# One bound per routed expert: every second expert's weights bounded by sums of absolute values on ScalarE, the others by the largest value on VectorE

## The reference

```python
H = einsum('btd,od->bto', x, W)
delta = einsum('btr,bor->bto', einsum('btd,brd->btr', x, A[idx]), Bm[idx]) * scalings[idx]
c = H + delta
shared = sum over 2 experts of gelu(c @ Wsh_up) @ Wsh_down
probs = softmax(c @ W_router); gate = the 2 largest of 16 probabilities
routed = sum over 16 experts of (gelu(c @ Wrt_up) * gate) @ Wrt_down
out = x + shared + routed
```

## Time and profile before

| | before |
|---|---|
| median of 3 runs | 685.81 us (685.29 to 686.54) |
| span of the profiled execution, first to last instruction | 679.9 us |
| PE, DVE, ACT, POOL busy | 627.5, 457.4, 327.2, 222.6 us |
| mean granted TensorE clock | 0.974 of full speed |
| bytes moved, mean rate | 135.68 MB, 200 GB/s |

### The profile page before, as it was taken

One profiled execution on the slowest core, in us unless ns is written; L12 is line 12 of the kernel. 1 busy time (PEld: TensorE's weight loads), 2 busy tenths in 40 slices (PEclk: granted clock), 3 DMA queues, 4 the chain that ended last, 5 costly groups with the idle time before them and its releaser, 6 DMA issues.

```text
span 679.9 us, 13742 instructions
## 1 busy us (share of the span) xinstructions
PE 627.5 (92%) x4115; PEld 428.4 (63%) x4117; DVE 457.4 (67%) x900; ACT 327.2 (48%) x480; POOL 222.6 (33%) x288
## 2 busy tenths in 40 slices
PE   4998999999989758889999999999999999989794
PEld 2465656566657435556777777777777777665561
DVE  2779999999974998525555555555555554688674
ACT  1333224677775743464555555555555554333230
POOL 1000000101012742373333333333333306777771
PEclk9997999999998988999999999999999999999898
DMA  7688994343334312165555555555555539989966
GB/s 275 281 312 286 374 346 168 123 157 142 132 127 128 124 63 93 32 217 171 159 159 169 161 154 159 164 168 157 156 159 167 164 107 377 366 301 362 369 205 248
DMA packets 49765, 135.68 MB, mean 200 GB/s; under 512 B 6160, under 2 KB 6288, under 8 KB 47312
## 3 DMA queue, kind: packets, MB, share of 16 engines
q1 hardware_dynamic: 38304, 97.93, 39.1%
q0 software_dynamic: 11440, 37.50, 20.0%
HBM read 86.38 MB, written 49.02 MB: 199 GB/s over the span
## 4 chain that ended last, share of the span: by engine, by line
PE 53%; DVE 17%; POOL 12%; issue 7%; DMA 7%; ACT 1%; SPq 0%; DVEq 0%; POOLq 0%; ACTq 0%
PE bank L1412 15%; PE bank L1393 14%; POOL rtw L608 9%; PE bank L1249 7%; PE bank L1377 5%; DVE lot_max L906 5%; DMA act_in<-xT 3%; PE bank L1402 2%; PE bank L1327 2%; PE bank L1257 2%; PE bank L1274 2%; DMA region<-xc_dram,slot_idx 2%; PE bank L1238 1%; DVE x_max L947 1%; PE bank L1265 1%
## 5 line engine op out<-in xcount | busy, mean ns | idle before, releaser
L1129 DVE SCALAR_TENSOR_TENSOR region<-bank,scale,region 128x512 f16<-128x512 f32 x79 | 59.2, 751 | 128.7 <-ACT region L809 128.7
L1393 PE MATMUL bank<-rtw,region 128*128 x948 | 116.4, 273 | 0.0
L1412 PE MATMUL bank<-rtw,tmp 128*128 x474 | 115.2, 379 | 0.6 <-DVE tmp L1137 0.6
L1393 PEld LDWEIGHTS bank<-rtw,region 128*128 128x128 f16 x948 | 92.8, 98 | 10.1
L1340 PE MATMUL bank<-shw,hid 128*128 128x512 f16 x384 | 91.3, 397 | 8.3 <-DVE rtw L1193 7.7
L574 POOL DMA_INDIRECT region<-xc_dram,slot_idx x79 | 77.1, 976 | 61.3 <-POOL slot_idx L571 61.3
L1327 PE MATMUL bank<-act_in,shw 128*128 128x256 f16 x768 | 89.4, 277 | 2.9 <-ACT tmp L756 1.7
L1327 PEld LDWEIGHTS bank<-act_in,shw 128*128 128x128 f16 x768 | 75.8, 100 | 16.0 <-ACT tmp L756 2.2
L816 ACT ACTIVATE region<-bank,un_dn 128x512 f32<-128x512 f32 x79 | 54.3, 687 | 57.3 <-PE bank L1412 54.8
L608 POOL DMA_INDIRECT rtw<-r_dram,row_idx x64 | 70.0, 1093 | 27.6 <-issue 14.8
L1340 PEld LDWEIGHTS bank<-shw,hid 128*128 128x128 f16 x384 | 38.4, 102 | 56.4 <-issue 10.0
(11 more groups left out here) (157 smaller groups left out, 910.0 us busy)
## 6 DMA issues: line engine op xcount, KB each, us to landing
r_dram<-region SPq DMA_DIRECT2D x79, 256.0 KB
rtw<-rt_w SPq DMA_DIRECT2D x16, 1024.0 KB, 7.4
act_in<-xT SPq DMA_DIRECT2D x16, 512.0 KB, 3.8
xc_dram<-rows SPq DMA_DIRECT2D x16, 512.0 KB, 3.7
xcT_dram<-hid SPq DMA_DIRECT2D x16, 512.0 KB, 2.8
rtw<-x_rows SPq DMA_DIRECT2D x16, 512.0 KB, 5.4
rtw<-xcT_dram SPq DMA_DIRECT2D x13, 512.0 KB, 6.1
out<-rtw SPq DMA_DIRECT2D x9, 512.0 KB, 5.6
```

The costliest lines, as they stand in the source:

```text
L1129: nc.vector.scalar_tensor_tensor(xgT[s][:, 1], R_XT[s][:].rearrange("p (k t) -> p k t", k=HK), col(scale, C_ALL).bitcast(F32), xgT[s][:, 0 ...
L1393: last = mm(R_UP[s][:, 0:D], xgT[s][:, xp, k, :], rtw[:, bass.ds(e, 1), w0:w0 + D].rearrange("p a d -> p (a d)"), start=(k == 0 and n == 0 ...
L1412: last = mm(R_DN[s][:], midT[s][:, xp, m, :], rtw[:, bass.ds(e, 1), w0:w0 + H].rearrange("p a h -> p (a h)"), start=(m == 0 and n == 0), s ...
```

## The change

The bounds of the odd experts are no longer the largest absolute values, found on DVE, but the sums of absolute values, taken on ACT (`lot_sums`: two `Abs` activations of 128 x 1024 with a sum along the row; the 16-bit absolute values themselves are written to a place that isn't used at the time). A sum of absolute values is never below the largest of them, so the scale stays a valid one, and the power of two is a smaller one. ACT counts its bounds in a semaphore of its own, `lot_sum_ready`, and SP waits for bound n in the semaphore of the engine that makes it. ACT's loop over steps 4 to 7 is written out. DVE's eight bounds are spread anew over its steps.

```diff
--- before.py
+++ after.py
@@ -249,8 +249,8 @@
 
         w_adapters, w_mask, w_cond, w_shared = sem("w_adapters"), sem("w_mask"), sem("w_cond"), sem("w_shared")
         w_loaded = sems("w_loaded", 4)
-        lot_max_ready, largest_ready, reduced, scale_ready, un_ready = (
-            sem("lot_max_ready"), sem("largest_ready"), sem("reduced"), sem("scale_ready"), sem("un_ready"))
+        lot_max_ready, lot_sum_ready, largest_ready, reduced, scale_ready, un_ready = (
+            sem("lot_max_ready"), sem("lot_sum_ready"), sem("largest_ready"), sem("reduced"), sem("scale_ready"), sem("un_ready"))
         w_half, w_split, c_chunk_ready = sem("w_half"), sem("w_split"), sem("c_chunk_ready")
         condT_loaded, condT_half, actT_ready = sems("condT_loaded"), sem("condT_half"), sem("actT_ready")
         hid_half, hid_ready = sem("hid_half"), sem("hid_ready")
@@ -372,7 +372,7 @@
                         sp.wait_ge(lin_split, 2)
                     if n + 5 == E_RT:
                         sp.wait_ge(w_split, 2)
-                    sp.wait_ge(lot_max_ready, n + 1)
+                    sp.wait_ge(lot_sum_ready if n % 2 else lot_max_ready, n // 2 + 1)
                     sp.dma_start(arrived(n + 5), rt_w[:, bass.ds(n + 4, 1), :].rearrange("p a n -> p (a n)")).then_inc(w_loaded[r], 16)
 
             for i in range(E_RT // 4 - 1):
@@ -664,6 +664,19 @@
                     last = nc.scalar.activation(src, src, ACT.Copy, scale=by)
                 last.then_inc(condT_half, 1)
 
+            def lot_sums(e):
+                i, r = e // 4, e % 4
+                act.wait_ge(w_loaded[r], 16 * (i + 1))
+                if e > E_RT // 2:
+                    act.wait_ge(w_split, 1)
+                if e > 1:
+                    act.wait_ge(lot_sum_ready, e // 2)
+                for u in range(2):
+                    place = rtw[:, 0 if e > E_RT // 2 else E_RT - 1, u * WU:(u + 1) * WU]
+                    last = nc.scalar.activation(place, arrived(e + 1)[:, u * WU:(u + 1) * WU], ACT.Abs,
+                                                accum_out=lot_max[:, u, e:e + 1])
+                last.then_inc(lot_sum_ready, 1)
+
             def high_linear(dst, src, n):
                 nc.scalar.activation(dst, src, ACT.Copy, scale=col(scale, n).bitcast(F32)).then_inc(lin_half, 1)
 
@@ -708,17 +721,25 @@
             cond_step(0, 1, first=True)
             high_x(3, 1)
             cond_T(1, 0, 1, first=True)
+            lot_sums(1)
             act.wait_ge(scale_ready, 2)
             high_shared(0)
             cond_rows(1, 0)
             high_x(4, 0)
             cond_T(2, 1, 0)
+            lot_sums(3)
             high_shared(1)
             cond_rows(1, 1)
-            with act.Fori(2, A_HALF // 2) as i:
+            for i in range(2, A_HALF // 2):
                 for s in range(2):
                     high_x(2 * i + s + 1, 1 - s)
-                    cond_step(i, s)
+                    cond_T(2 * i + s - 1, i - 1 + s, 1 - s)
+                    if i == 2:
+                        lot_sums(5 + 2 * s)
+                    else:
+                        for e in (9 + 4 * s, 11 + 4 * s):
+                            lot_sums(e)
+                    cond_rows(i, s)
             def routed_step(i, s, more=True):
                 c = 2 * i + s
                 if more:
@@ -1008,17 +1029,18 @@
             link(nc.vector.tensor_scalar(mask[:], mask[:], w_to_a[:], None, ALU.mult))
             x_largest(1, 0)
             x_scales(2, 0)
-            search_step(0, 1, [(0, 0), (0, 1)], masked=True)
+            search_step(0, 1, [(0, 0)], masked=True)
             scales(2, SH_UP, RT_UP)
-            search_step(1, 0, [(0, 2), (0, 3), (1, 0)])
-            search_step(1, 1, [(1, 1), (1, 2), (1, 3)])
+            search_step(1, 0, [(0, 2)])
+            search_step(1, 1, [(1, 0)])
             for i in range(2, A_HALF // 2):
                 for s in range(2):
-                    search_step(i, s, [(i, 2 * s), (i, 2 * s + 1)])
+                    search_step(i, s, [(1 + s, 2 - 2 * s)] if i == 2 else [(2, 2)] if s == 0 else [(3, 0), (3, 2)])
                     if i == 2:
                         low_shared(s)
             dve.wait_ge(c_chunk_ready, EARLY)
-            dve.wait_ge(lot_max_ready, E_RT)
+            dve.wait_ge(lot_max_ready, E_RT // 2)
+            dve.wait_ge(lot_sum_ready, E_RT // 2)
             nc.vector.tensor_reduce(largest[:, RT_UP:RT_DN + 1], lot_max[:], AX_X, ALU.max)
             nc.vector.tensor_reduce(col(largest, C_EARLY), c_chunk[:, 0:EARLY], AX_X, ALU.max).then_inc(largest_ready, 1)
             scales(3, RT_UP, C_ALL)
```

## The result

| | before | after |
|---|---|---|
| median of 4 runs each | 686.17 us (685.29 to 687.32) | 704.33 us (699.75 to 705.74) |
| ratio | | 1.0269, 95% interval 1.0225 to 1.0313 |
| span of the profiled execution | 679.9 us | 703.7 us |
| VectorE, ScalarE busy | 457.4, 327.2 us | 439.2, 343.3 us |
| start of PE's step 2, of step 15 | 37.00, 187.78 | 38.03, 207.15 |

The account below looks back on a forecast made before the run. A transfer relay, then DVE, then PE were taken to bound the kernel; a closed loop of 14.55 us per turn delays the scales by 13.6 us, plus 1.6 for the clock: 15.2 on 685.81 gives 701.0 us, range 693 to 709.

Parts of the forecast that it names:

- What bounds the kernel, and that only the end of the scales moves: Relay of transfers, then DVE, then PE at 10.86 us; the scales' end at 117.7 us shifts everything later.
- Parts 1 to 3 of the loop: Steps 2 to 6: x arrival to end of `cond_T` 5.94 us, `lot_sums` 2.2, SP's issues 0.4.
- Part 4, the transfer: In the loop, the next x chunk lands 6.0 us after issue behind a load; ends 5.0 and 7.1.
- x 9: Last x transfer, with two loads ahead: 8.8 us, landing at 122.6 us instead of 103.4.
- The clock: Around steps 8 and 9 PE's lower clock costs 1.6 of 3.5 us; inside the loop the loss is hidden.
- Rival D: Low clock makes PE join the loop, period 17 or 18 us, some 712 us in all; chance 0.14.
- The time around the span: Time outside the profiled span: 5.9 us, taking 695.1 to 701.0.
- B: Faster: x transfers are short and the relief of DVE counts, 678 to 684 us; chance 0.05.
- C: No difference: loop period near 12 us as loads and transfers overlap fully, 686 us; chance 0.03.
- A: The closed loop over steps 2 to 6 as summed, 693 to 709 us; chance 0.78.
- The signs: Expected in the changed trace, such as SP's loads behind ACT's sums, scales at about 131 us, DVE busy 18 us less.

Follow-up runs that it names:

- e9: Changed kernel, but in the first six chunks SP stores rows and transpose only once the x transfer ahead has landed: 695.52 us, ratio to before 1.0161.
- e1: Changed kernel, but SP issues the next x chunk ahead of the two bound waits and the two expert loads: 679.93 us, ratio to before 0.9916.
- e3: Changed kernel, but SP waits for the arrival of load n, not bound n, before issuing load n+4: 675.88 us, ratio to before 0.9877.
- e2: Changed kernel, but behind the wait for the odd bound SP issues the next x chunk before the 1 MB load: 685.09 us, ratio to before 0.9996.

## Why the prediction was right

It gave 701.0 us in a range of 693 to 709; measured are 704.3. The mechanism was the one forecast, but the number is nearer than its parts deserve. The scales were forecast 13.6 us later and came 19.4 us later, or 18.3 without the later start of step 2; and 1.6 us were put on the clock, which cost nothing. Without that term the sum is 699.4. By its own steps:

- *What bounds the kernel, and that only the end of the scales moves.* Right. The scales end 19.4 us later, of which 1.03 were there at the start of step 2 already. From the scales to the transposes of step 9 are 8.63 us in both kernels (117.73 to 126.36, 137.09 to 145.72), and the steps behind are 10.87 us. The stretch grew by 18.3 us and the time by 18.2. The 1.03 us are no more than what the start of step 2 differs by between profiles.
- *Parts 1 to 3 of the loop.* 5.94, 2.2 and 0.4 us were predicted and measured. The issue of x 4 was forecast at 45.1 us and came at 46.14, of which 1.03 is the later start.
- *Part 4, the transfer.* The term that was mis-sized: 6.0 us predicted, 7.03, 6.79, 6.87, 6.85 and 6.97 measured, a mean of 6.9. Five of them make 4.5 us. I had reckoned with the load ahead and taken the other load as gone, which it was, but left the two stores behind x out; e9 puts 1.1 us on them. The trace of before had a near case that the sum didn't use, an x transfer with a load 0.4 us ahead and both stores within 1 us behind (a second load, issued at 52.78, was still under way). Its line in the chain, and the two stores among SP's issues:

```profile
55.67 7.02 DMA act_in<-xT
...
56.15 0.43 SPq L361 DMA_DIRECT2D xc_dram<-rows  x1
56.62 0.54 SPq L363 DMA_DIRECT2D xcT_dram<-hid  x1
```

The x transfer of the earlier trace rows, 7.1 us, which I had taken as the upper end because of traffic ahead of it, also had a store 0.5 us behind it (issued at 67.21, against 66.73). The Trainium skill says in "DMA: Bandwidth & Descriptors", "Queues, rings and completion order", that descriptors are consumed in ring order; read as first in, first out, that would make the stores behind x free, and e9 shows that they weren't. The same section says that a later descriptor may finish its write before an earlier one; no run here shows that.
- *x 9.* 8.8 us predicted, 8.53 measured.
- *The clock.* I had put 1.6 us on it, and nothing of it is on the path: the 8.63 us above are unchanged. PE's adapter products behind the scales (L1279) did take 3.57 us there, against 1.96 at the full clock, but PE's wait for its rows behind them shrank from 1.29 to 0.46 us. The lower clock came in more than one step, as forecast (two of the windows, columns as in the earlier trace rows; the clock is the third figure from the end):

```profile
60.00:64.00 4.00, 4.00 (x16) 3.48 (x17) 0.99 (x1) 3.22 (x5) 0.00 (x0) 0.50 0.65 211
...
108.00:112.00 4.00, 4.00 (x8) 1.56 (x9) 1.48 (x3) 2.99 (x6) 0.00 (x0) 0.50 0.88 270
```

PE waited in each turn anyway, 1.03 to 2.87 us ahead of its router products. Rival D didn't come: the four parts add up to the whole turn of 15.4 us, and PE isn't among them.
- *The time around the span.* I took 5.9 us, the median less the profile's span. The execution profiled after took 705.68 us with a span of 703.7, so it is 2.0, and by the same 2.0 the profiled execution of before was one of about 682, faster than any of the four in the table above. Since the sum is a difference on top of the median, the error cancelled.
- *The rivals.* B was ruled out by the arrivals; e1 and e3 show that its gain, up to 8 us by my sum for PE's pace, was to be had once the loop was cut (9.5 us in the stretch). C would have needed transfers of 3.6 to 4.0 us. e2 made them 3.4 to 4.8 us, and the result was indeed no difference.
- *Slips in the sums.* The upper end of A is 24.6 us on 685.8, which is 710 and not 709, and five periods of 3 us on the forecast make 716 for D, not 712. The four parts are 14.54, not 14.55. None of this touches the forecast.
- *The signs.* Met were SP's order behind the sums, the pair at 2.2 us, the lower clock more than once and DVE's 18 us. Missed, mainly for the two reasons above (longer transfers, later start), were the arrivals 14 to 15 us apart (15.4 to 15.5), the scales at about 131 (137.1) and PE's steps 9 to 15 starting 14 to 16 us later (19.4 to 20.2). `x_largest` was idle for 5.4 to 8.3 us, where 4 to 7 were named.

What stays open: the profiled execution after is 4.4 us longer than that of before from the start of step 15 on (496.5 against 492.1 us), which the timed runs don't show as a difference of the kernels; other profiles have 489 to 500 us there.

## What to carry to other kernels

Before moving work off a busy engine, follow the signal that the work gives: if a queue that issues in order waits for it, everything queued behind the wait inherits the new place of the work, and a wait that was harmless because its signal came early can close a loop when the signal comes just in time. Write the loop down with its parts (here 5.94 + 2.2 + 0.4 + 6.9 us) and compare its turn with the step of the engine that is to be relieved; the relief counts only below that. And where such a wait only keeps order or pace, wait for what is really needed (here the arrival of an earlier load): it turned a loss of 18.2 us into a gain of 8.6 and, timed again, 11.5.

## What the runs showed of the hardware that I had not expected

- A transfer of 512 KB took 6.9 us with a 1 MB load issued 0.4 us ahead and two 512 KB stores 0.5 and 1.0 us behind it, 5.6 to 5.8 us without the stores (e9), and 3.4 to 4.8 us with the load and the stores behind it (e2). So what is issued behind a transfer slows it too, here by 1.1 us; the load ahead cost it more: an estimate from 5.7 us without the stores and the 3.4 us of the earlier trace rows with nothing ahead is 2.3 us.
- A sum along the row on ACT adds a separate instruction of 0.20 us to each `Abs`, of which about 0.1 shows at the end of a pair (76.60 to 76.70); two `Abs` of 128x1024 with their sums took 2.2 us, no more than two scaled copies.
- PE's lower clock, present in several steps of the loop, cost nothing that the length of the stage shows, because PE was waiting in each turn anyway.
